# Projections of batches 1 to 3 and their evacuations issued earlier in the first eleven steps, weight casts moved behind tanh, and one weight chunk instead of two in the third step

## The reference

```
q = ctx @ Wq.T + bq ;  k = ctx @ Wk.T + bk
scores = (q @ k.T) / sqrt(128) * layernorm(x)          # [b, 512, 512], masked
x2 = x + softmax(scores)
xn = layernorm(x2)
logits = xn @ router_w ; the two best of 8 experts per row, weight = sigmoid(logit)
out = x2 + silu(xn @ sg) * (xn @ su) @ sd               # shared expert
         + for each chosen expert: silu(p xn @ gate) * (p xn @ up) @ down
```

## Time and profile before

| | |
|---|---|
| median of 3 runs | 351.07 us (350.42 to 351.41) |
| the profiled execution's own time | 350.65 us |
| its span, first to last instruction | 348.6 us |
| granted TensorE clock, mean | 0.978 of full |
| busy share of the span | PE 91%, POOL 58%, DVE 60%, ACT 52% |

### The profile page before, as it was taken

One profiled execution on the slowest core, in us unless ns is written; L12 is line 12 of the kernel. 1 busy time (PEld: TensorE's weight loads), 2 busy tenths in 40 slices (PEclk: granted clock), 3 DMA queues, 4 the chain that ended last, 5 costly groups with the idle time before them and its releaser, 6 DMA issues.

```text
span 348.6 us, 6707 instructions
## 1 busy us (share of the span) xinstructions
PE 318.9 (91%) x1715; PEld 228.3 (65%) x1715; DVE 210.3 (60%) x450; ACT 182.5 (52%) x416; POOL 202.4 (58%) x203
## 2 busy tenths in 40 slices
PE   7659997998999899779999999999999999999991
PEld 6336675775777567546777777777777777777760
DVE  0996776998699879964744445444445444445440
ACT  2567886877686853425544434444434444434430
POOL 0886999887578610193635385755466565545333
PEclk9969999999999999899999999999999999999997
DMA  6947699755474541084554666866766576675735
GB/s 184 320 126 255 231 307 255 216 207 197 149 253 126 179 154 11 0 254 148 93 116 69 115 115 104 160 117 117 122 106 107 98 125 118 98 126 91 114 38 85
DMA packets 29763, 50.62 MB, mean 145 GB/s; under 512 B 5472, under 2 KB 9312, under 8 KB 29728
## 3 DMA queue, kind: packets, MB, share of 16 engines
q0 software_dynamic: 9008, 21.66, 34.6%
q1 hardware_dynamic: 19760, 28.01, 25.4%
q10 hardware_dynamic: 960, 0.53, 0.7%
HBM read 30.45 MB, written 19.73 MB: 144 GB/s over the span
## 4 chain that ended last, share of the span: by engine, by line
PE 79%; DVE 7%; ACT 6%; issue 3%; DMA 2%; POOL 0%; SPq 0%; DVEq 0%; ACTq 0%; POOLq 0%
PE bank L1054 14%; PE bank L1010 13%; PE bank L1015 10%; PE bank L1075 6%; PE bank L1081 6%; PE bank L1078 6%; PE bank L1193 5%; PE bank L1063 3%; PE bank L973 3%; PE bank L1032 2%; PE bank L982 2%; DMA xin<-in_x 2%; PE bank L967 2%; PE bank L1043 1%; PE bank L1039 1%
## 5 line engine op out<-in xcount | busy, mean ns | idle before, releaser
L459 POOL DMA_INDIRECT out_rows<-y,jscatter x39 | 62.2, 1595 | 69.9 <-DMA out_rows<-y,jscatter 38.2
L1054 PE MATMUL bank<-gu_hi,x_lo 128*128 (+1 forms) x220 | 71.9, 448 | 0.9 <-DVE x_lo L703 0.9
L1010 PE MATMUL bank<-gu_hi,x_hi 128*128 (+1 forms) x220 | 63.9, 412 | 1.8 <-ACT x_hi L527 0.9
L440 POOL DMA_INDIRECT xg<-xn_rows,jgather x39 | 41.9, 1075 | 34.0 <-DVE jgather L871 15.3
L535 ACT CAST h_hi<-bank 128x256 fp32r<-128x256 f32 x55 | 20.5, 372 | 61.0 <-PE bank L1063 57.6
L1054 PEld LDWEIGHTS bank<-gu_hi,x_lo 128*128 128x128 f32 x220 | 41.2, 189 | 17.1 <-issue 3.8
L922 DVE SCALAR_TENSOR_TENSOR h<-bank,xg,h 128x256 f32<-128x256 f32 x39 | 18.9, 484 | 53.6 <-ACT h L630 50.6
L1010 PEld LDWEIGHTS bank<-gu_hi,x_hi 128*128 128x128 f32 x220 | 40.9, 190 | 13.1 <-issue 4.6
L703 DVE TENSOR_TENSOR x_lo<-bank,x_hi 128x512 fp32r<-128x512 f32 x55 | 37.9, 690 | 14.8 <-ACT x_bf L528 13.7
L1015 PE MATMUL bank<-gu_lo,x_bf 128*128 (+1 forms) x172 | 44.7, 383 | 0.0
L630 ACT ACTIVATE h<-bank,xg 128x256 f32<-128x256 f32 x39 | 18.5, 474 | 49.9 <-PE bank L1054 48.7
(11 more groups left out here) (147 smaller groups left out, 566.4 us busy)
## 6 DMA issues: line engine op xcount, KB each, us to landing
stage<-in_L_ffn_gate_up_w SPq DMA_DIRECT2D x16, 512.0 KB, 4.1
xin<-in_x SPq DMA_DIRECT2D x16, 256.0 KB, 4.8
xn_rows<-xn SPq DMA_DIRECT2D x16, 256.0 KB, 4.0
stage<-in_L_ffn_down_w SPq DMA_DIRECT2D x8, 512.0 KB, 4.0
out_rows<-x SPq DMA_DIRECT2D x16, 256.0 KB, 4.2
out_rows<-zeros POOLq DMA_DIRECT2D x1, 1024.0 KB, 6.9
ctx_in<-in_ctx SPq DMA_DIRECT2D x1, 768.0 KB, 8.4
xg<-xn_rows,jgather POOLq DMA_INDIRECT x39
```

The lines of the kernel that those rows point to most:

```text
L440: g.indirect_dma_start(out=xg[:, r, :], out_offset=None, in_=xn_dram, in_offset=bass.IndirectOffsetOnAxis(ap=jgather[:, n - TILES:n - TILE ...
L459: g.indirect_dma_start(out=out, out_offset=bass.IndirectOffsetOnAxis(ap=jscatter[:, n - TILES:n - TILES + 1], axis=0), in_=y[:, r, :], in_ ...
L1010: tn.matmul(ps_g(n)[:], x_hi[:, n % TS, k, :], gu_hi[:, e, k, :], start=(k == 0), stop=False)
L1054: last = tn.matmul(ps_g(n)[:], x_lo[:, n % TS, k, :], gu_hi[:, e, k, :], start=False, stop=(k == KC - 1))
```

## The change

1. `BOUNDS`: step 2 has one chunk (3), steps 3 to 7 have two each (4, 5; 6, 7; 8, 9; 10, 11; 12, 13). From step 8 on the table is the same.
2. ACT: the first chunk of a step with two is cast behind tanh. In step 2 chunk 3 is still cast ahead of tanh.
3. ACT: the evacuations of batch 1's projections stand right behind tanh in step 2, those of batch 2 right behind `normal` in steps 5 and 6, those of batch 3 right behind `normal` in steps 9 and 10.
4. PE: in step 2 the two projections of batch 1 stand right behind `gate_up_rest(0)`, ahead of `scores(3)`. The PE places of batches 2 and 3 stay.

```diff
-BOUNDS = (0, 2, 3, 5, 7, 9, 11, 13, 14, 15, 16, 17, 18, 19, 20, 21, 21)
+BOUNDS = (0, 2, 3, 4, 6, 8, 10, 12, 14, 15, 16, 17, 18, 19, 20, 21, 21)
...
                     normal(s - 1)
+                if s in (5, 6):
+                    projection(2, s - 5)
+                if s in (9, 10):
+                    projection(3, s - 9)
...
                 if j >= 0:
-                    for c in chunks(s)[1:]:
-                        high_part(c - 1)
+                    if s == 2:
+                        high_part(3)
                     half_tanh(j)
-                    if len(chunks(s)) == 1:
-                        high_part(chunks(s)[0])
+                    if s == 2:
+                        projection(1, 0)
+                        projection(1, 1)
+                    else:
+                        for c in chunks(s)[0:1]:
+                            high_part(c)
                     x_high(s - 1)
                     if s < TILES - 1:
                         h_high(j)
                         chosen_exp(j)
-                    if s == 2:
-                        projection(1, 0)
-                        projection(1, 1)
                     for c in chunks(s)[1:]:
                         high_part(c)
-                    if s in (5, 6):
-                        projection(2, s - 5)
-                    if s in (9, 10):
-                        projection(3, s - 9)
...
                 if j >= 0:
                     gate_up_rest(j, SHARED)
+                if s == 2:
+                    projection(1, 0)
+                    projection(1, 1)
...
-                if s == 2:
-                    projection(1, 0)
-                    projection(1, 1)
```

## The result

The changed kernel took 349.78 us (median of 12 runs, 347.92 to 351.10), the kernel before, timed beside it, 351.38 us (12 runs, 350.42 to 354.56). The ratio is 0.9948 with a 95% interval of 0.9924 to 0.9973: 1.8 us faster, 0.9 to 2.7. The forecast had 348.7 with a gain of 2.3 and a range of 346.4 to 350.2. Run once more in a later session (e10), the same kernel had 348.89 against 351.71, ratio 0.9904 (0.9869 to 0.9939). The two ratios of one kernel differ by 0.4%, or 1.5 us: so the runs alone don't tell kernels of different sessions apart by less.

A forecast was written before the change was run, and what follows sets the result against it. PE sets most of the pace, with POOL next: PE's ceiling of 2.67 + 0.37 + 1.74 + 0.6 = 5.4 us shrinks to 2.3 through POOL. 350.65 - 2.3 = 348.35, plus 0.42 for the median, gives 348.7; range 346.4 to 350.2.

The forecast's parts named there:

- a: `projection(2, 1)` in step 5: PE's wait for the late evacuation on ACT and its restart go, worth 2.67 us.
- c: `projection(3, 1)` in step 9: 1.5 us of PE's wait and 0.24 of restart go, worth 1.74 us.
- b: `scores(8)` on PE: its short wait behind a late evacuation and the restart go, worth 0.37 us.
- d: Steps 2 to 4: the moved projections cover PE's waits for `h` and `x_lo`, worth 0.6 us, bounds 0 and 0.7.
- POOL becomes the bound: Steps 7 to 9: POOL's lateness leaves a gain of 2.3 us, time 348.7; the forecast case, chance 0.5.
- rival 2: POOL isn't the bound, its early idles being shorter; PE gains 3.3 to 5.4 us; chance 0.2.
- Starts or durations: POOL from low part 8 to 14: 24.0 us timed start to start, 23.1 by durations, which would give gain 3.2.
- The waits for `xn`: PE at `xn_transpose` between 60 and 81 us: two or three new waits behind POOL's `nmr`, 3 us together.
- The course of the gain: Gain rises to 3.5 us at step 7, falls to 0.55 at step 9's transpose, then is 2.3 after step 9.
- The clock: On PE: neither the removed waits nor the new ones of at most 1.4 us carry a clock change.

The follow-up runs named there:

- e10: The changed kernel again, unaltered, in a later session; 348.89 us against 351.71 for the kernel before, ratio 0.9904.
- e4: The changed kernel with `pair_inv_std` ahead of the first low part on POOL in steps 6, 7 and 8; ratio 0.9892 to the kernel before.
- e8: e9 with the old table of chunks; ratio 0.9829 to the kernel before.
- e9: e4 with the tile load ahead of the first weight load in SP's queue in steps 6, 7 and 8; ratio 0.9863 to the kernel before.
- e5: The kernel before with step 2's part alone: batch 1's projections ahead of `scores(3)`, their evacuations behind tanh; ratio 0.9999.
- e2: The changed kernel with the old table of chunks, casts still behind tanh; ratio 0.9912 to the kernel before.
- e1: The kernel before with only the evacuations of batches 2 and 3 moved right behind `normal`; ratio 0.9943 to the kernel before.
- e3: The changed kernel with the first cast of a two-chunk step ahead of tanh again, new table kept; ratio 0.9924 to the kernel before.
- e7: The kernel before with step 2's part, early evacuations of batches 2 and 3, and `pair_inv_std` first in steps 6 to 8; ratio 0.9929.

## Why the prediction held, point by point

- **a and c, the two stalls.** Right: no wait of L968 is left in the trace after, and the two steps are 2.65 and 1.66 us shorter (forecast 2.67 and 1.74).
- **b, `scores(8)`.** It was to be worth 0.37. In the changed kernel it isn't visible by itself: the step that holds it also has the wait for tile 6, and is 0.55 longer. In e4, e8 and e9, where that wait is gone, the step is 0.32 to 0.33 shorter than before.
- **d, steps 2 to 4.** Forecast 0.6. From `xn_transpose(2)` to `(4)` the change saves 0.45. The part ahead depends on when the clock comes back (last section); at equal clock it saves about 0.45 more, an estimate. So d is 0.9, above its own bound of 0.7. Step 2's part alone (e5) has 0.67; the rest comes with the new table and cast order. Timing can't confirm either.
- **POOL becomes the bound.** Right, and e4 shows it as the cause, not only as a neighbour in time. Forecast idles before low parts 4, 6 and 8: 2.3, 1.2, 0.6; measured 2.87, 0.55, 0.89, and 1.83, 0.55, 0.84 in e10. These sizes are off, but the forecast doesn't rest on them: it starts from low part 8. And POOL had not simply worked ahead before, since it idled 2.10 ahead of low part 4. Forecast from low part 8 to low part 14: 24.0; measured 74.55 - 50.50 = 24.05. The sign named for rival 2, low part 14 before 73, didn't come.

```profile
50.50:74.55 24.05, 22.05 (x129) 16.14 (x129) 19.69 (x46) 20.05 (x43) 23.16 (x34) 1.00 0.79 232
```

- **Starts or durations.** POOL is busy 23.16 of these 24.05 us although it waits for nobody in them. The sum by durations would have been 23.1, and short by 0.9; the start-to-start sum is right, as the Trainium skill has it ("Perfetto Trace Analysis", "GPSIMD Engine Instruction").
- **The waits for `xn`.** Forecast 0.4 and 1.4 for tiles 6 and 7 and 3 in all, which leaves 1.2 for tile 8; measured 0.77, 1.23, 0.97, in all 2.97.
- **The total.** Forecast 2.3. The ruler has 1.77 from step 3 on and some 0.45 ahead of it, 2.2; the runs say 1.8 (0.9 to 2.7), and in the second session 3.4 (2.2 to 4.6). The course of the gain fits too: with the 0.45, it is 3.5 at `xn_transpose(5)`, 0.6 at `(8)` and 2.2 at `(9)`, against 3.5, 0.55 and 2.3. Two slips in the sum change little: the cast of chunk 8 ends at 49.98 + 0.3 + 0.95 = 51.23, not 51.25 or 51.27, and 80.72 for PE's arrival at `xn_transpose(8)` is the chain's time, where the timeline has 80.55.
- **What it missed.** That the waits come from POOL was right, but not that the change's own table makes a good part of them: it costs 1.1 us (e2). And that the early evacuations need the cast behind tanh: with a cast ahead of tanh as well, PE has waits for `h` of some 0.3 each instead (e1, e3, e7).
- **The clock.** The new waits of up to 1.23 us left the granted clock at 1.00 in all stretches shown, as forecast. The prediction's words that the trace shows no fall for "the longest wait here" hold for stall a (2.4 us) only: in the same trace PE waits 4.0 us ahead of `xn_transpose(0)`, and the granted clock is 0.63 from 19 to 21 us and 0.50 from 21 to 23.

## What to carry to other kernels

Before a stall is moved out of one engine's queue, look how full the next engine is over the same stretch: what it lacks is given back, here 3.0 of 5.4 us. Work on an in-order engine that was done early is a store that covers later load; here a change that makes it wait in steps 3 to 5 is paid in steps 7 to 9. And put what others wait for (`nmr`, a tile load) ahead of the bulk work in its queue, but look also what is then queued behind: in e7 a tile's load came late for it, and in e9 the weight load did, so that the step bought nothing; e8, which had the old table as well, was the shortest.

## What wasn't expected of the hardware

The spread between runs of one kernel, 3 us, is larger than the change. Part of it is TensorE's granted clock. In all traces PE idles 4.0 us ahead of `xn_transpose(0)`, and the clock falls to 0.50 (1.2 GHz) before it. When it is back at 1.00 (2.4 GHz) differs from execution to execution, for the same kernel too. The changed kernel, first trace and then e10, granted clock in the third column from the end; `xn_transpose(0)` starts at 20.63 and at 22.18:

```profile
23.00:25.00 2.00, 2.00 (x6) 0.99 (x5) 1.97 (x5) 1.97 (x4) 1.89 (x5) 0.50 0.79 162
25.00:27.00 2.00, 2.00 (x8) 1.28 (x7) 1.28 (x4) 2.00 (x4) 1.83 (x1) 0.74 0.60 231
```

```profile
23.00:25.00 2.00, 2.00 (x9) 1.58 (x8) 1.90 (x6) 1.67 (x3) 1.45 (x3) 0.50 0.23 9
25.00:27.00 2.00, 2.00 (x9) 1.21 (x8) 1.95 (x6) 1.97 (x6) 1.90 (x5) 0.89 0.81 246
```

From the clock's share in the second row, the clock is back at about 26.0 and 25.4, that is 5.4 and 3.3 us after `xn_transpose(0)`. From there to `xn_transpose(2)` it took 35.11 - 20.63 = 14.48 and 35.62 - 22.18 = 13.44. Over the ten traces with the new step 2 this is one line, from 13.29 us when the clock is back 2.9 us after, to 14.83 us when it is back 6.2 us after. The kernel before and e1, with the old step 2, took 14.55 with the clock back after 4.7 and 4.4; the line has 14.1 and 14.0 there, which is where the 0.45 of d comes from. A second place is between 120 and 150 us, where the first trace of the changed kernel was granted 1.00, 0.93 and 0.90 in the three tens, and e10 0.89, 0.94 and 0.75.

The larger part lies behind the stretch. The spans of these two traces are 345.8 and 349.0, 3.2 apart: 0.51 of it stands at the start of `xn_transpose(2)` (35.11 and 35.62), since e10 came later to `xn_transpose(0)` but had the shorter way from there; 0.03 in the stretch; and 2.66 behind it (253.06 and 255.72 from `xn_transpose(10)` to the end). Over all twelve traces `xn_transpose(2)` starts between 34.64 and 36.57, and what lies behind the stretch, where the kernels do the same work, takes 253.0 to 255.9. How much of these 2.9 us the clock makes wasn't separated.
